# Retention layer plus FP4 linear layer on one core: v projected token-major from the second group on, with a new order on VectorE and new loads for two weight slots

## What is computed

```python
q, k, v = heads((x @ Wq + bq) * scaling), heads(x @ Wk + bk), heads(x @ Wv + bv)
ret = jnp.einsum('bhid,bhjd->bhij', q, k) * D[None]      # D: causal, decays with the distance
scale = jnp.clip(jnp.abs(ret.sum(-1, keepdims=True)), 1.0, None)
attn = jnp.einsum('bhij,bhjd->bhid', ret / scale, v)
g = group_norm(attn) * gn_w + gn_b                       # over each head's 64 features
return silu(x @ Wg + bg) * g @ Wo + bo
...
xq, xs, _ = quantize_nvfp4(x2d, x_tensor_scale)          # ffn: x and weight rounded to FP4 in blocks of 16
out = jnp.einsum('mbk,nbk->mn', xq * xs, wq * ws) * output_scale + bias
```

## Time and profile before

| | us |
|---|---|
| median of three runs | 2140.41 |
| the profiled execution, its time | 2142.48 |
| the profiled execution, its span | 2140.7 |
| TensorE busy (matmul) | 2080.3 (97%) |
| VectorE busy | 1541.7 (72%) |
| ScalarE busy | 685.9 (32%) |
| GpSimd busy | 640.0 (30%) |
| mean granted TensorE clock | 0.991 of full |

### The profile page before, as it was taken

How to read it: one execution, slowest core, us unless ns; L and a number is a source line. 1 busy time by engine, 2 the same in 40 slices (tenths; PEclk the granted TensorE clock), 3 DMA queues, 4 the chain that set the end, 5 groups by cost and what they waited for, 6 DMA issues and landing times.

```text
span 2140.7 us, 51098 instructions
## 1 busy us (share of the span) xinstructions
PE 2080.3 (97%) x18098; PEld 1053.5 (49%) x18098; DVE 1541.7 (72%) x4375; ACT 685.9 (32%) x1318; POOL 640.0 (30%) x456
## 2 busy tenths in 40 slices
PE   5988899999999999999999999999999999999999
PEld 3444444455455454555555555454555454555444
DVE  7899898988889877566767556767656767656732
ACT  5756623332223233322323322323322322322300
POOL 1323232332233333223332223233223233223220
PEclk8999999999999999999999999999999999999999
DMA  8878634334343443323333323333323333223343
GB/s 317 282 253 265 218 98 138 108 109 136 100 127 108 137 128 94 102 83 109 124 103 93 103 84 109 122 103 94 103 85 107 122 103 95 103 86 106 122 153 117
DMA packets 181686, 275.61 MB, mean 129 GB/s; under 512 B 117344, under 2 KB 117472, under 8 KB 181344
## 3 DMA queue, kind: packets, MB, share of 16 engines
q1 hardware_dynamic: 181600, 274.48, 39.8%
HBM read 204.18 MB, written 40.89 MB: 114 GB/s over the span
## 4 chain that ended last, share of the span: by engine, by line
PE 86%; DVE 11%; DMA 2%; issue 1%; ACT 0%; SPq 0%; DVEq 0%; ACTq 0%
PE mm L1288 54%; PE mm L1223 10%; PE tp L1223 6%; PE mm L1232 4%; PE tp L1298 3%; PE four L1338 3%; PE four L1351 2%; PE tp L1326 1%; PE four L1311 1%; PE four L1232 1%; PE tp L1251 1%; DVE wo L929 1%; DMA res<-in_w_f 1%; DMA parts<-wo 1%; DVE state L1041 1%
## 5 line engine op out<-in xcount | busy, mean ns | idle before, releaser
L1288 PE MATMUL mm<-xnT,wring 128*128 128x512 f16 x6144 | 1365.8, 381 | 13.8 <-DVE wring L929 6.8
L1288 PEld LDWEIGHTS mm<-xnT,wring 128*128 128x128 f16 x6144 | 598.2, 98 | 710.3 <-issue 25.2
L695 ACT ACTIVATE work<-four,gs 128x64 f32<-128x64 f32 x512 | 158.1, 414 | 554.2 <-DVE gs L1068 554.2
L556 POOL TENSOR_TENSOR yT<-gn,gate 128x512 f32 (+1 forms) x64 | 84.2, 1315 | 800.6 <-ACT gn L706 800.6
L1223 PE MATMUL mm<-wo,yT 128*128 128x512 f16 x960 | 214.1, 380 | 0.1
L1055 DVE BATCH_NORM_STATS2 gst<-four 128x6 f32<-128x64 f32 x512 | 73.5, 216 | 195.0 <-PE four L1351 194.8
L539 POOL TENSOR_TENSOR qparts<-qT,qparts 128x512 f16<-128x512 f32 x64 | 77.0, 1203 | 363.2 <-ACT qT L664 363.1
L539 POOL TENSOR_TENSOR kparts<-kT,kparts 128x512 f16<-128x512 f32 x64 | 84.2, 1316 | 225.1 <-ACT kT L664 225.1
L1223 PEld LDWEIGHTS mm<-wo,yT 128*128 (+1 forms) x960 | 91.0, 98 | 108.3 <-issue 0.2
L1223 PE MATMUL tp<-wo,yT 128*128 128x512 f16 x576 | 128.2, 379 | 0.0
L662 ACT ACTIVATE qparts<-mm,consts,down 128x512 f16<-128x512 f32 x64 | 49.7, 776 | 213.2 <-PE mm L1288 213.2
(11 more groups left out here) (198 smaller groups left out, 2648.8 us busy)
## 6 DMA issues: line engine op xcount, KB each, us to landing
wring<-parts SPq DMA_DIRECT2D x252, 512.0 KB, 3.9
xt<-in_x SPq DMA_DIRECT2D x34, 512.0 KB, 3.6
out<-res SPq DMA_DIRECT2D x32, 512.0 KB, 3.0
parts<-wo SPq DMA_DIRECT2D x28, 512.0 KB, 5.6
res<-in_x SPq DMA_DIRECT2D x28, 512.0 KB, 3.5
ftile<-in_w_f SPq DMA_DIRECT2D x12, 512.0 KB, 4.4
parts<-wring SPq DMA_DIRECT2D x8, 512.0 KB, 6.8
probs<-in_x SPq DMA_DIRECT2D x5, 512.0 KB, 4.6
```

What stands on the lines that cost most here:

```text
L556: nc.gpsimd.tensor_tensor(hi, gn[:], gate[:, u], ALU.mult)
L695: last = nc.scalar.activation(work[:, c * P + h * HD:c * P + (h + 1) * HD], ao[h][:, c * VW:c * VW + HD], ACT.Identity, bias=gs[:, 1, g:g ...
L1288: last = MM(mm[n % 2][:], wring[:, n, wj, k, :], xnT[:, parity, xj, k, :], start=(j == 0), stop=(j == 3 * KT - 1))
```

## The change

From SECOND on, v is no longer projected as vT and transposed. `project_v(j)` makes v token-major for both pairs at once: for each of two 128-token chunks, 24 matmuls with a 128x128 tile of `xnT` stationary and 256 columns of weights moving, which are slots 1 and 3 of `wring` side by side. Two calls (j = 0, 1) cover the 512 tokens. ScalarE's `evacuate_v(j)` scales the result into `v1`, which now has room for four heads, in two operations of 128x256; GpSimd's `bias_v(j)` adds the bias of v to it, one operation of 128x512, two a body; `state_increments` waits for both (`v_ready`). `transpose_kv` of v and `copy_v` are left out. In the place of `project(0, 1)` comes `project_v(0)`, in that of `project(0, 3)` comes `project_v(1)`, and in that of `project(1, 1)` comes `project(0, 3)`.

Slots 1 and 3 hold v of both pairs until `project_v(1)` is done. Then `load_gates` loads g of both pairs into them, and after `project(0, 3)` and `project(1, 3)` `load_v` brings v of the next two pairs. The number of loads is the same. In FIRST a 512 KB copy inside DRAM and a 512 KB load of the bias are added in the second body.

On VectorE `mask_scores(0)` now stands between the two halves of the quantization of x, in all phases from SECOND on. In SECOND and THIRD f_half(0) goes from before group_norm(0) to before states(1), f_half(1) to behind emit_half(0), and emit_half(1) and emit_done come ahead of group_norm(1).

```diff
 def bank_uses(phase):
-    t0 = ("k0", "u0", "v1", "u1", "g1")
-    t1 = ("v0", "k1", "g0")
+    if phase == FIRST:
+        t0, t1 = ("k0", "u0", "v1", "u1", "g1"), ("v0", "k1", "g0")
+    else:
+        t0, t1 = ("k0", "u0", "u1", "g1"), ("k1", "g0")
...
+                def load_ring(n, matrix, pair):
+                    src = a["parts"][matrix, ds(pair, 1)].rearrange("a p n -> p (a n)")
+                    sp.dma_start(wring[:, n].rearrange("p a b c -> p (a b c)"), src)\
+                      .then_inc(s["w_" + MATS[n]], 16)
+                def load_gates():
+                    w("mm1_full", 2)
+                    for u in range(2):
+                        load_ring(2 * u + 1, 3, q * 2 + u)
+                def load_v(u):
+                    w("mm1_full", g_use(phase, u))
+                    load_ring(2 * u + 1, 1, q * 2 + 2 + u)
...
+                def bias_v(j):
+                    w("mm1_free", j + 1)
+                    pool.sem_inc(pool_turn, 1)
+                    out = v1[:, 2 * j:2 * j + 2, :, 0:HD]
+                    rows = v_bias[:, ds(q * (2 * P), 2 * P)].rearrange("p (h d) -> p h d", d=HD)
+                    nc.gpsimd.tensor_tensor(out, out, rows.unsqueeze(1).broadcast_to([P, 2, 4, HD]), ALU.add)\
+                      .then_inc(s["v_ready"], 1)
...
                 split(1, kT[:], kparts)
+                if phase != FIRST:
+                    bias_v(0)
                 split(2, qT[:, 0], qparts)
                 decay_q(0)
                 x_lo()
+                if phase != FIRST:
+                    bias_v(1)
                 split(3, kT[:], kparts)
...
+                def evacuate_v(j):
+                    w("within", 0)
+                    w("mm1_full", j + 1)
+                    act.sem_inc(act_turn, 1)
+                    for u in range(2):
+                        from_u = mm[1][:].rearrange("p (c a h d) -> p c a h d", c=2, a=2, d=HD)[:, :, u]
+                        last = nc.scalar.activation(v1[:, 2 * j:2 * j + 2, 2 * u:2 * u + 2, 0:HD], from_u,
+                                                    ACT.Copy, scale=down[:, 1, pair(u)])
+                    last.then_inc(s["mm1_free"], 1)
...
                 evacuate(0, 0)
-                evacuate(0, 1)
+                evacuate_v(0)
                 affine(1, 1)
                 x_hi()
                 evacuate(0, 2)
-                copy_v(0)
                 decay_k(0)
+                evacuate_v(1)
+                evacuate(1, 0)
                 evacuate(0, 3)
-                evacuate(1, 0)
-                evacuate(1, 1)
                 decay_k(1)
                 evacuate(1, 2)
-                copy_v(1)
...
                 quantize_half(xt, 0)
+                mask_scores(0)
                 quantize_half(xt, 1)
-                mask_scores(0)
                 if phase in QUANTIZE:
                     f_scales()
                 states(0)
-                if phase in QUANTIZE:
-                    f_half(0)
                 group_norm(0)
                 mask_scores(1)
                 if phase in QUANTIZE:
-                    f_half(1)
+                    f_half(0)
                 states(1)
                 emit_half(w, 0, "mm0", 5)
                 if phase == MIDDLE:
                     emit_linear(w, 0, "mm1", 5, "mm0", 5)
-                group_norm(1)
-                if phase in QUANTIZE:
+                else:
+                    f_half(1)
                     emit_half(w, 1, "mm1", 5)
                     emit_done(w, "mm1_free", 5)
+                group_norm(1)
...
+                def project_v(j):
+                    if j == 0:
+                        w("w_v", 0)
+                        w("w_g", 0)
+                    w("mm1_free", j)
+                    out = mm[1][:].rearrange("p (c a x) -> p c a x", c=2, a=2)
+                    for c in range(2):
+                        tokens = slice((2 * j + c) * P, (2 * j + c + 1) * P)
+                        n = 0
+                        for k in range(KT):
+                            for wj, xj in ((0, 0), (1, 0), (0, 1)):
+                                last = MM(out[:, c], xnT[:, parity, xj, k, tokens], wring[:, 1::2, wj, k, :],
+                                          start=(n == 0), stop=(n == 3 * KT - 1))
+                                n += 1
+                    last.then_inc(s["mm1_full"], 1)
```

More of the change, by code:

```diff
@@ L480, in body @@
                     return
-                for n in range(4):
-                    load_slice(0, n)
+                load_slice(0, 0)
+                load_slice(0, 2)
+                load_gates()
                 move_x_parts()
@@ L485, in body @@
                 load_x(1)
-                for n in range(4):
-                    load_slice(1, n)
+                load_slice(1, 0)
+                load_v(0)
+                load_slice(1, 2)
+                load_v(1)
                 w("out_ready", 1)
@@ L591, in _ @@
             for phase in (FIRST, SECOND, THIRD, MIDDLE, TAIL):
+                if phase == SECOND:
+                    pool.wait_ge(v_bias_in, 16)
                 run_phase(pool, phase, body)
@@ L702, in affine @@
                     bk, use = bank_uses(phase)[f"g{u}"]
-                    w(f"t{bk}_full", use - 5 * back)
+                    w(f"t{bk}_full", 0 if back else use)
                     w("gated", u - 2 * back)
@@ L1277, in project @@
                 def project(u, n):
-                    use = mm_use(u, n)
+                    use = g_use(phase, u) if n == 3 else mm_use(u, n)
+                    slot = n
+                    if n == 3 and phase != FIRST:
+                        slot = 2 * u + 1
                     if (phase, i, u) == (FIRST, 0, 0):
@@ L1287, in project @@
                         for wj, xj in ((0, 0), (0, 1), (1, 0)):
-                            last = MM(mm[n % 2][:], wring[:, n, wj, k, :], xnT[:, parity, xj, k, :],
+                            last = MM(mm[n % 2][:], wring[:, slot, wj, k, :], xnT[:, parity, xj, k, :],
                                       start=(j == 0), stop=(j == 3 * KT - 1))
@@ L1313, in scores, with v_head @@
                     last.then_inc(s["scores_full"], 1)
+                def v_head(u, h):
+                    return h if phase == FIRST else 2 * u + h
                 def state_increments(u):
                     bk, use = uses[f"u{u}"]
-                    for which in "kv":
+                    for which in ("kv" if phase == FIRST else "k"):
                         b, n = uses[f"{which}{u}"]
                         w(f"t{b}_free", n)
+                    if phase != FIRST:
+                        w("v_ready", 2)
                     w(f"t{bk}_free", use - 1)
@@ L1325, in state_increments @@
                         for h in range(2):
-                            last = MM(increment(bk, k)[h * HD:(h + 1) * HD], kn[rows, c, h, :], v1[rows, c, h, :],
+                            last = MM(increment(bk, k)[h * HD:(h + 1) * HD], kn[rows, c, h, :], v1[rows, c, v_head(u, h), :],
                                       start=True, stop=True)
@@ L1360, in body @@
                     sum_slices(0, 4, 4)
-                project(0, 1)
+                if phase == FIRST:
+                    project(0, 1)
+                else:
+                    project_v(0)
                 if phase != FIRST or i:
@@ L1364, in body @@
                 project(0, 2)
-                transpose_kv(0, "v", vT, 1)
+                if phase == FIRST:
+                    transpose_kv(0, "v", vT, 1)
                 transpose_kv(0, "k", kT, 0)
-                project(0, 3)
+                if phase == FIRST:
+                    project(0, 3)
+                else:
+                    project_v(1)
                 project(1, 0)
@@ L1375, in body @@
                     sum_slices(i + 1, 0, SLICES)
-                project(1, 1)
+                if phase == FIRST:
+                    project(1, 1)
+                else:
+                    project(0, 3)
                 if phase == FIRST and i == 0:
@@ L1386, in body @@
                 attend_earlier(0)
-                transpose_kv(1, "v", vT, 1)
+                if phase == FIRST:
+                    transpose_kv(1, "v", vT, 1)
                 project(1, 3)
```

54 lines of the change are left out of this document (34 added, 20 removed), and 4 rows, old and new, of the table PER.

## The result

The changed kernel takes 2125.58 us (median of 4 runs, 2123.72 to 2129.73), the kernel before 2140.66 on the same chip (4 runs). The medians differ by 15.1 us. The ratio is 0.9940, 95% interval 0.9926 to 0.9955, which is a gain of 10 to 16 us, 13 at its middle. The forecast was 2128.7 us, a gain of 11.7. The profiled execution took 2123.72 us, with a span of 2121.9.

The account below looks back on a forecast made before the run. TensorE was taken to bound the kernel, with a VectorE bound close behind in SECOND and THIRD. MIDDLE's -16.2 and SECOND and THIRD's +4.5 gave -11.7 us, from 2140.41 to 2128.7 us, range 2114 to 2142.

Parts of the forecast that it names:

- TensorE's work and MIDDLE: Transposes removed, matmuls at 109.2 ns: -0.81 us a body for TensorE, -16.2 us over MIDDLE's 20 bodies.
- I cost these at nothing: MIDDLE: ScalarE's swapped operations, GpSimd's bias_v and the wait for mm1 ahead of project_v(0) were to add no time.
- The loop in SECOND: SECOND and THIRD: waits through group_norm(1) and ScalarE's evacuation to project(0, 2) make the period 62.0 us, now 61.16.
- the predicted 1.8 us of waiting: SECOND and THIRD: TensorE's wait for ScalarE's kT ahead of project(0, 2), about 1.8 us.
- Seven periods at +0.8: SECOND and THIRD: after SECOND's first body, seven periods each lose 0.8 us, +5.6 us.
- the way into MIDDLE: From attend_earlier(0) to project(0, 2) into MIDDLE: 32.7 us instead of 31.5, +1.2 us.
- The first body, -2.3: SECOND's first body: the earlier mask leaves TensorE held by states(0) alone, so attend_earlier(0) starts 2.3 us sooner.
- The sum: SECOND and THIRD together, from first body, seven periods and the way into MIDDLE: +4.5 us.
- VectorE's loop does not bind: Rival: SECOND and THIRD gain as well if contention in group_norm(0) falls away; -25.8 us, 2114 us, chance 0.16.
- The late gate tile: Rival: in MIDDLE project(0, 3) waits 0.3 to 1.2 us a body for its load; 2135 to 2153 us, chance 0.15.
- The exposed weight load: Rival: 256-column matmuls no longer hide their weight loads; 5.2 us a body, 145 us in all, 2285, chance 0.07.
- the upper end of 63.4: SECOND and THIRD: upper end of the period from VectorE's own sum, with contention from bias_v and the split of k.

Follow-up runs that it names:

- The order alone: Kernel before with only VectorE's blocks in the changed kernel's order, v still projected feature-major and transposed: 2139.34 us, ratio 1.0002.

## Why the prediction was right, and where its steps were off

- **TensorE's work and MIDDLE**: right. 109.2 ns a matmul, -0.82 us a body (-0.81), MIDDLE -15.8 to -16.0 us (-16.2 with 20 bodies). No wait of any kind appeared there.
- **"I cost these at nothing"** for bias_v in MIDDLE: right only because the mask had been moved. With the mask in its old place MIDDLE is 24 us longer. The step had named the wait for v as the danger and not the one for `probs`, which is VectorE's. That MIDDLE came out as forecast is, in this respect, luck: the diff had moved the mask, and my working gave that no part in MIDDLE.
- **The loop in SECOND**: right in kind and size. 61.83 against 62.0, and the waits stand ahead of project(0, 2). Of the predicted 1.8 us of waiting only 0.6 is seen there, and 0.5 ahead of attend_earlier(0): the loop's slack was spread over two waits, and attend_earlier(0) too was a little late.
- **"Seven periods at +0.8"**: mis-sized. SECOND has +0.9 in its first period, behind the wait of 3.38 us, and +0.65 to +0.7 in the next three; THIRD has none, 61.05 to 61.15 against 61.14 to 61.20. I had read one body, of SECOND, and used it for both. In THIRD the first instruction of states is a copy from PSUM, not the SBUF copy of 0.94 us (1.26 in the earlier trace rows), and one state operation less runs. The order alone shows the same step (62.24 and 61.6); that these two differences make it is argued, no run tests it. The seven periods and the way into MIDDLE came to +2.5 and +2.6 us, by the two pairs of profiles, where 5.6 + 1.2 = 6.8 was forecast.
- **The first body, -2.3**: the mask's gain is there with the order alone, but bias_v takes 2.6 us back, so it came to 0 to +1.0. I had put bias_v's contention into the range of the period and not into this term.
- **The sum** for SECOND and THIRD was +4.5 and measured +2.6 and +3.5: two errors of opposite sign, so that the sum came nearer than its terms, which is luck. Altogether the phases give -12.5 and -13.2 us against -11.7; the medians -15.1 and -13.8.
- **Rivals.** That VectorE's loop does not bind is refuted: the period is 61.83 and falls to 60.65 when VectorE is relieved of 2.8 us. The late gate tile didn't occur, and would cost more than I said. The exposed weight load doesn't exist at 256 columns nor at 128. Its price was also added up wrongly: 145 us more than the forecast is 2274 us, and the 2285 was counted from the time before.
- **Contention.** The Trainium skill (SBUF — State Buffer, "Who interferes with whom") put the forecast some 8 us higher by its exclusive lock. This case's traces agree on the lock, as the copy of 2.33 us beside an addition of 2.35 shows, and the price was paid where VectorE has no slack: 2.6 us in the first body of SECOND, where the two bias_v take 1.17 and 1.36. In a later body VectorE is busy 1.5 us longer, but that falls into the 1.91 us for which it would wait for the scores. So the period came out at 61.8 and not at the upper end of 63.4, for a reason that my working did not have.

## What to carry to other kernels

When work is moved to a helper engine, the price can appear on the engine whose operations then wait for the helper's (VectorE's for GpSimd's here), and the reorder that comes along in the diff may be what pays for it: cost each reorder with and without the other parts. Before a period is multiplied, read a body of every phase, since one instruction (a copy from SBUF here, from PSUM there) can decide. Where VectorE must run beside GpSimd, let GpSimd's long operation start just behind the last SBUF-to-SBUF instruction and beside those that read PSUM; one instruction's difference in that start was worth 13 us here.

## What the runs showed of the hardware that was not expected

- Weight loads of 98 ns were fully hidden behind matmuls at 55.8 ns apiece (128 columns), 109.2 (256) and 215.8 (512).
- After waits of 2.72 and 4.37 us TensorE's granted clock averaged 0.75 to 0.76 over the next 24 matmuls, which took 6.9 us instead of 5.2, so that such a wait costs 1.7 us more than the view of waits shows. The wait of 3.38 us in the changed kernel's first body of SECOND shows the same: the 24 matmuls behind it take 7.04 us. The waits of 0.5 and 0.6 us in SECOND cost nothing beyond themselves, nor did one of 1.64 us in the run without the bias: 5.35 us behind them.
- VectorE's SBUF-to-SBUF copy of 128x65 took 2.33 us beside a GpSimd addition of 2.35 and 0.20 without it, while its operations with an input in PSUM kept 0.28 us beside the same addition.
- FIRST, in which the granted clock averaged 0.95 and 0.97 in two profiles of one kernel, took 268.5 and 262.5 us in them, and 262 to 269 in all: a spread as large as the effect of many an edit, which only cutting the span by phases takes out.
